# Queries and keys turned by transposing DMAs, and maxima over 1024 keys from two double banks

## The chip, the core and the metric

One core of a Trainium2 chip runs the whole kernel in one launch. Its engines work side by side, each through its own list of instructions, and meet at semaphores: TensorE (PE; PEld is its weight load), VectorE (DVE), ScalarE (ACT), GpSimd (POOL), and SyncE (SP), which here only issues DMAs. The metric is the device time of the kernel in microseconds; lower is better.

## What is computed

A transformer layer on 8 sequences of 1024 tokens of width 256: layer norm, attention with 16 heads of 16 channels (rotary embedding on the last 256 tokens), a residual; then layer norm, a mixture of 16 experts in which each expert takes its 128 best tokens of a sequence, a shared expert, a residual. The change touches the attention alone:

```python
q = (x @ wq + bq); k = x @ wk; v = x @ wv + bv        # [8, 16 heads, 1024, 16]
q, k = apply_rope(q, k, cos, sin)                     # in bfloat16
scores = einsum('bhqd,bhkd->bhqk', q, k) / 4
out = softmax(scores) @ v @ wo + bo
```

## The kernel before

The attention runs first (until about 1510 us), then the shared expert, then the others. All instructions of an engine stand in one order that is written out by hand in the code, in steps. A batch (one sequence) has 64 steps, numbered S = 0 to 63; V counts them over all batches. Four heads make a group; a group and one half of its 1024 queries make a unit of 8 steps, one for each tile of 128 keys. QUAD = 32 channels are kept for a head, of which 16 hold the query or key and three more hold the negative of the row's maximum, split into three bfloat16 parts, so that the turned scores come out of the matmul already less their maximum.

Each step V does four things.

- Rows of scores (`score_rows`, L742): for 128 queries of one head against 512 keys, into one of the three `ring` banks. VectorE takes the maximum over the 512 keys (`maximum`, L460). Four rows a step, 32 a unit, LEAD = 12 steps ahead of their use. VectorE joins the two halves of the keys (`join_halves`, L467), POOL splits the maxima into `QP` (`split_maxima`, L299).
- Turned scores (`score_turned`, L754): four a step, one for each head j (called ex 0 to 3), 128 keys against 512 queries, into the rotating banks `rot`; ScalarE takes their exp into `PR` (L575).
- Values (`weigh_values`, L765): the products of step V - 2, four heads on four column strips, into the bank `pv`.
- Work beside (`beside`, L81, by the table `BESIDE`): projections q, k, v of the next batch, the output projection and gates of the batch before, transposes of activations (`xt`, `aot`, `x2t`), and the transposes of queries and keys: `qT` turns a group's queries or keys by eight TensorE transposes (L707) that ScalarE copies out (L596), `q2` turns a unit's queries again once their maxima are in (L714, L605). In every eighth step the finished output of a unit is turned too (`ot`). ScalarE copies a unit's `pv` bank out before that (`evacuate`, L627).

A head's matmul of scores uses 32 rows of the array (`tile_position`, strip j), and in each half of a step PE issues two rows of scores and two turned scores for four different heads:

```python
score_rows(m); score_rows(m + 1)          # heads 2, 3
score_turned(V, 0); score_turned(V, 1)
weigh_values(V - LAG)
score_rows(m + 2); score_rows(m + 3)      # heads 0, 1
score_turned(V, 2); score_turned(V, 3)
for item in beside(V): fill(item)
```

All exps and all work beside share the rotating banks in one sequence (`ORDER`, L102): item n uses bank n % ROT, ROT = 4, and PE waits until ScalarE has emptied item n - ROT (`bank`, L659). A row of scores m waits in the same way for the maximum of row m - RING (L749). SP loads and stores whole batches as soon as their semaphores allow (L250).

Of the kernel before, what the change touches and what calls it, by code (L numbers as in the profile page):

```python
# [43 lines left out]
def attention(nc, d, ident, SC, B):  # L44
# [12 lines left out]
    ROT = 4  # L57
    RING = 3
    P_STEPS = 3
    LAST = B * STEPS  # L60
    CHECKS = 32 * UNITS * B
# [4 lines left out]
    BESIDE = {0: (-1, "aot", 0, 0), 1: (-1, "aot", 1, 0), 2: (0, "qT", 2, 0), 3: (0, "v", 7), 4: (0, "qT", 2, 1),  # L66
              5: (-1, "proj", 0), 6: (0, "q2", 1), 7: (-1, "aot", 0, 1), 8: (-1, "aot", 1, 1), 9: (-1, "proj", 1),
              10: (-1, "proj", 2), 11: (-1, "proj", 3), 12: (-1, "proj", 4), 13: (-1, "proj", 5), 14: (0, "q2", 2),
# [9 lines left out]
    FIRST = {61: (1, "v", 0), 52: (1, "v", 1), 53: (1, "v", 2), 55: (1, "v", 3), 56: (1, "qT", 1, 0), 57: (1, "qT", 1, 1),  # L78
             58: (1, "v", 4), 59: (1, "v", 5), 60: (1, "v", 6), 62: (1, "q2", 0)}

    def beside(V):  # L81
# [7 lines left out]
        if S in table:  # L89
# [4 lines left out]

    HEAD = ([("xt", 0, h, half) for half in range(2) for h in range(KH)]
            + [(n, 0, i) for i in TILES for n in ("q", "k")]
            + [("qT", 0, 0, 0), ("qT", 0, 0, 1), ("bo",)])
# [13 lines left out]
    def check(m):  # L111

        unit, n = m // 32, m % 32
        return unit, (2, 3, 0, 1)[n % 4], n // 4 % 2, 4 * (unit % 2) + n // 8

    ctx = ExitStack()
    with ctx:
# [6 lines left out]
        identb = sb("identb", [P, P], BF16)  # L124
# [19 lines left out]
        QP = [sb(f"QP{n}", [P, TT, NH, QUAD], BF16) for n in range(2)]  # L144
        KP = sb("KP", [P, TT, NH, QUAD], BF16)
# [10 lines left out]
        MX = sb("MX", [P, 2, 2, 4, 4], F32)  # L156
# [12 lines left out]
        rt1 = sb("rt1", [P, ROPE_TILES, NH, HD], BF16)  # L169
        rt2 = sb("rt2", [P, ROPE_TILES, NH, HD], BF16)  # L170
# [31 lines left out]
        maxima_ready = sem("maxima_ready")  # L202
# [15 lines left out]
        def _(sp):  # L218
# [28 lines left out]

            sp.dma_start(XR[:], rows("x", 0)).then_inc(xr_in, 16)
            load_next(1)
            for b in range(B):  # L250
                if b:
                    store_x1(b - 1)
                if b + 2 < B:
                    load_next(b + 2)
                if b:
                    store_xn2(b - 1)
                    sp.wait_ge(x1_out, 16 * b)
                    sp.wait_ge(xn2_out, 16 * b)
                    sp.dma_start(XR[:], rows("x", b)).then_inc(xr_in, 16)
# [6 lines left out]
        def _(pool):  # L266
# [9 lines left out]
            def rope(b):  # L276

                pool.wait_ge(rot_done, done(("k", b, 7)))
                pool.wait_ge(q_biased, TT * b + 2)
                for n, A in enumerate((QP[b % 2], KP)):  # L280
                    if n:
                        pool.wait_ge(rope_done, 2 * b + 1)
                    a = A[:, TT - ROPE_TILES:TT, :, 0:HD]
                    h = HD // 2

                    def over(c, lo, hi):
                        return c[:, :, lo:hi].unsqueeze(2).to_broadcast([P, ROPE_TILES, NH, hi - lo])
                    nc.gpsimd.tensor_tensor(rt1[:], a, over(cosb, 0, HD), ALU.mult)
                    nc.gpsimd.tensor_tensor(rt2[:, :, :, 0:h], a[:, :, :, h:HD], over(sinb, 0, h), ALU.mult)
                    own.inc(nc.gpsimd.tensor_tensor(rt2[:, :, :, h:HD], a[:, :, :, 0:h], over(sinb, h, HD), ALU.mult))  # L290
                    own.wait(pool)
                    nc.gpsimd.tensor_tensor(a, rt1[:], rt2[:], ALU.add).then_inc(rope_done, 1)

            def clear_maxima(b):

                own.inc(nc.gpsimd.memset(QP[b % 2][:, :, :, HD:HD + 3], 0.0))
                own.wait(pool)
# [124 lines left out]
        def _(dve):  # L422
# [87 lines left out]
            for V in range(-LEAD, LAST):  # L510
# [6 lines left out]
                if m < CHECKS:  # L517
                    maximum(m + 2)
                    maximum(m + 3)
                    if m % 32 == 28:  # L520
                        join_halves(m // 32)
# [837 lines left out]
```

## Time and profile before

| what | us |
|---|---|
| time before, median of 3 runs | 2411.47 (2410.88 to 2412.66) |
| the profiled execution: its time | 2413.08 |
| its span, first to last instruction | 2411.3 |
| PE, DVE, ACT, POOL busy | 2272.7, 1864.4, 1630.3, 1098.7 |
| maxima (L464), 2048 of 512 keys | 1283.6 busy |
| exps (L575), 2048 | 1121.6 busy |

The busy times are unions over the span. PE's is of little use by itself, since matmuls overlap and their ends are modelled; starts are what to compare. VectorE and ScalarE are busy nearly all the time in the attention and half of it later.

### The profile page before, as it was taken

The page shows a single profiled execution, that of the slowest core. Times are in us where ns is not written, and L with a number is a line of the kernel's source. Part 1 is how long each engine was busy: PE and PEld are TensorE (multiplying, and loading weights), DVE is VectorE, ACT ScalarE, POOL GpSimd, SP SyncE. Part 2 cuts the span into 40 slices and gives each one's busy share as a digit, 9 for nine tenths or more (in the row PEclk, how much of TensorE's full clock was granted, in tenths as well). Part 3 has the DMA queues.
Part 4 walks back from the last instruction along what each step waited for, and adds up shares of the span by engine and source line. Part 5 has one row for each costly group of instructions (what it writes and reads, how often), then busy time and mean ns, then how long its engine had stood idle before and what let it go on. Part 6 is the DMA issues. An engine that isn't in the chain of part 4 may idle for free. (4 is left out here: it accounts for less than half of the span.)

```text
span 2411.3 us, 43902 instructions
## 1 busy us (share of the span) xinstructions
PE 2272.7 (94%) x16398; PEld 1335.3 (55%) x16398; DVE 1864.4 (77%) x3234; ACT 1630.3 (68%) x3168; POOL 1098.7 (46%) x1321
## 2 busy tenths in 40 slices
PE   5899999999999999999999997899997999999996
PEld 4233334334334334343344323788886888888886
DVE  5999999999999999999999993556564554555553
ACT  2699999999999999999999986323232343433332
POOL 4152573673573563663663342000004666666664
PEclk8799999999999999999999999899998999999998
DMA  2000011010020010010010010423223445454443
GB/s 76 1 19 1 1 36 36 1 54 19 4 67 3 19 53 1 19 54 1 19 36 1 19 36 27 140 79 104 79 70 90 103 109 113 83 114 111 105 96 36
DMA packets 104363, 122.74 MB, mean 51 GB/s; under 512 B 7553, under 2 KB 91393, under 8 KB 104193
## 3 DMA queue, kind: packets, MB, share of 16 engines
q1 hardware_dynamic: 79616, 86.90, 11.4%
q0 software_dynamic: 24576, 33.57, 8.0%
q8 instruction: 107, 1.75, 0.3%
q14 instruction: 64, 0.52, 0.1%
HBM read 78.50 MB, written 41.94 MB: 50 GB/s over the span
## 5 line engine op out<-in xcount | busy, mean ns | idle before, releaser
L464 DVE TENSOR_REDUCE sb_MX<-ring 128x1 f32<-128x512 f32 x2048 | 1283.6, 684 | 88.7 <-PE ring L751 66.1
L575 ACT ACTIVATE sb_PR<-rot 128x512 f32<-128x512 f32 x2048 | 1121.6, 620 | 89.1 <-PE rot L762 78.0
L773 PE MATMUL pv<-sb_PR,sb_VA 128*32 128x512 f32 x4096 | 547.1, 606 | 2.9 <-ACT sb_OT L630 0.6
L751 PE MATMUL ring<-sb_KT,sb_QT 32*128 32x512 bf16 x2048 | 508.3, 391 | 41.6 <-DVE sb_MX L464 29.0
L751 PEld LDWEIGHTS ring<-sb_KT,sb_QT 32*128 32x128 bf16 x2048 | 125.2, 91 | 619.5 <-DVE sb_MX L464 551.8
L762 PE MATMUL rot<-sb_QT,sb_KT 32*128 32x512 bf16 x2048 | 422.7, 386 | 1.6
L1064 ACT ACTIVATE ex_GL<-ex_gu 128x512 f32<-128x512 f32 x128 | 76.5, 598 | 347.2 <-PE ex_gu L41 345.0
L1131 DVE TENSOR_TENSOR ex_HF<-ex_GL,ex_gu 128x512 f32<-128x512 f32 x128 | 87.5, 683 | 250.7 <-ACT ex_GL L1064 250.7
L985 POOL TENSOR_TENSOR ex_pool_scratch<-identity 128x1 f32<-128x1 f32 x96 | 35.1, 366 | 459.8 <-POOLq L828 314.7
L1028 POOL DMA_INDIRECT out<-ex_YS,ex_rows_out x128 | 209.2, 1634 | 44.1 <-issue 43.5
L39 PE MATMUL ex_gu<-ex_XH,weights_high 128*128 128x512 f32 x512 | 200.4, 391 | 2.4 <-DVE ex_XL L1123 2.4
L40 PE MATMUL ex_gu<-ex_XL,weights_high 128*128 128x512 f32 x512 | 200.0, 391 | 0.0
L41 PE MATMUL ex_gu<-ex_XH,weights_low 128*128 128x512 f32 x512 | 199.9, 390 | 0.0
L366 POOL TENSOR_TENSOR sb_RD<-sb_AR,sb_minus_one 128x16 f32<-128x16 f32 x64 | 186.2, 2909 | 19.3 <-ACT sb_AR L610 19.3
L305 POOL CAST sb_QP<-sb_MX 128x16 bf16<-128x16 f32 x64 | 16.4, 256 | 378.6 <-DVE sb_MX L470 378.6
L1064 ACT ACTIVATE sh_GL<-sh_gu 128x512 f32<-128x512 f32 x64 | 38.2, 597 | 177.2 <-PE sh_gu L41 177.2
L39 PE MATMUL ex_y<-weights_high,ex_HH 128*128 128x256 f32 x512 | 148.2, 289 | 2.9 <-DVE ex_HL L1135 2.9
L773 PEld LDWEIGHTS pv<-sb_PR,sb_VA 128*32 128x32 f32 x4096 | 80.7, 108 | 124.4 <-issue 70.3
L40 PE MATMUL ex_y<-weights_low,ex_HH 128*128 128x256 f32 x512 | 145.5, 284 | 0.0
L41 PE MATMUL ex_y<-weights_high,ex_HL 128*128 128x256 f32 x512 | 145.5, 284 | 0.0
L1006 POOL DMA_INDIRECT ex_XG<-xn,ex_rows_in x128 | 126.0, 985 | 40.2 <-issue 39.6
L39 PE MATMUL rot<-sb_WH,sb_XH 128*128 128x256 f32 x384 | 129.0, 336 | 14.7 <-DVE sb_XL L458 4.8
(165 smaller groups left out, 4279.3 us busy)
## 6 DMA issues: line engine op xcount, KB each, us to landing
sb_XA<-x SPq DMA_DIRECT2D x8, 1024.0 KB, 5.7
sb_XR<-x SPq DMA_DIRECT2D x8, 1024.0 KB, 5.5
out<-sb_XR SPq DMA_DIRECT2D x8, 1024.0 KB, 4.5
xn<-sb_XN SPq DMA_DIRECT2D x8, 1024.0 KB, 4.5
sh_XG<-xn SPq DMA_DIRECT2D x16, 512.0 KB, 5.4
sh_X<-out SPq DMA_DIRECT2D x16, 512.0 KB, 4.9
weights<-WgT SPq DMA_DIRECT2D x16, 512.0 KB, 4.2
weights<-WuT SPq DMA_DIRECT2D x16, 512.0 KB, 5.9
```

What stands on the lines that cost most here:

```text
L39: nc.tensor.matmul(out, a_hi, b_hi, start=first, stop=False)
L40: nc.tensor.matmul(out, a_hi, b_lo, start=False, stop=False)
L41: return nc.tensor.matmul(out, a_lo, b_hi, start=False, stop=last)
L366: own.inc(nc.gpsimd.tensor_tensor(RD[:], AR[:, :, HD], minus_one[:], ALU.pow))
L464: nc.vector.reduce_max(MX[:, unit % 2, half, j, qt % 4:qt % 4 + 1], ring[m % RING][:], AX.X).then_inc(ring_done, 1)
L575: out = nc.scalar.activation(PR[V % P_STEPS][:, j, :], R[:], ACT.Exp, scale=0.25)
L751: nc.tensor.matmul(ring[m % RING][:], QT[g][r, P * qt:P * qt + P], KT[g][r, 512 * half:512 * half + 512], start=True, stop=True, tile_posi ...
L762: nc.tensor.matmul(R[:], KT[g][r, P * kt:P * kt + P], QT[g][r, 512 * qh:512 * qh + 512], start=True, stop=True, tile_position=(r.start, 0) ...
L773: out = nc.tensor.matmul(pv_bank[head(j), :], VA[b % 2][:, kt, 4 * g + j, :], PR[V % P_STEPS][:, j, :], start=(kt == 0), stop=(kt == TT - 1))
L1006: nc.gpsimd.indirect_dma_start(out=XG[k % 2][:, t, :], out_offset=None, in_=d["xn2"], in_offset=bass.IndirectOffsetOnAxis(ap=rows_in[:, b: ...
L1028: nc.gpsimd.indirect_dma_start(out=d["out"], out_offset=bass.IndirectOffsetOnAxis(ap=rows_out[:, b:b + 1], axis=0), in_=YS[k % 2][:, t, :] ...
L1064: nc.scalar.activation(GL[f % 2][:], gu[f % 2][:, 0, 0:N], ACT.Gelu).then_inc(gelu_ready, 1)
```

## The change

- A `ring` bank becomes a double bank: `score_rows` writes the two halves of the keys by two matmuls, one after the other, and `maximum` runs over 1024. There are 16 rows a unit and two a step, so one in each half step: of head 2 or 3 in the first, of head 0 or 1 in the second. `join_halves` goes.
- Two double banks (RING = 2) take four of the eight PSUM banks; the rotating banks become three (ROT = 3).
- The items `qT` and `q2` go from TensorE and ScalarE. SP issues transposing DMAs instead: `turn_qk` for the keys and queries of a group, `turn_whole` for the queries of a unit with their maxima. `QP` and `KP` are laid out by group for that.
- SP's other loads and stores get places among the turns, in the order of the steps. Rope on POOL runs tile by tile (16 instructions for 8). ScalarE's first key copy, POOL's split and clear, and PE's scores wait for turns.

```diff
-    ROT = 4
-    RING = 3
+    ROT = 3
+    RING = 2
-    CHECKS = 32 * UNITS * B
+    CHECKS = 16 * UNITS * B
     (BESIDE and FIRST lose their "qT" and "q2" entries; the others keep their steps)
+    TURN = {47: 0, 51: 1, 55: 2}
     def check(m):
-        unit, n = m // 32, m % 32
-        return unit, (2, 3, 0, 1)[n % 4], n // 4 % 2, 4 * (unit % 2) + n // 8
+        unit, n = m // 16, m % 16
+        return unit, (2, 0, 3, 1)[n % 4], 4 * (unit % 2) + n // 4
-        ring = [ctx.enter_context(nc.psum_tensor(f"ring{i}", [P, 512], F32)) for i in range(RING)]
+        ring = [ctx.enter_context(nc.psum_tensor(f"ring{i}", [P, 2, 512], F32)) for i in range(RING)]
+            def turn_qk(b, g):
+                sp.wait_ge(rope_done, 4 * (b + 1))
+                sp.wait_ge(q_biased, TT * (b + 1))
+                sp.wait_ge(rot_done, done(("k", b, TILES[-1])))
+                if b:
+                    sp.wait_ge(rot_done, done(("ex", (b - 1) * STEPS + 16 * g + 15, 3)))
+                for A, to in ((KP, KT), (QP[b % 2], QT)):
+                    sp.dma_start_transpose(to[g][:].rearrange("p (t c) -> p t c", c=P),
+                                           A[:, g].rearrange("p t j c -> p (t j c)")).then_inc(qk_turned[g], 16)
+            def turn_whole(unit):
+                b, n = unit // UNITS, unit % UNITS
+                g, qh = n // 2, n % 2
+                sp.wait_ge(parts_ready, unit + 1)
+                sp.dma_start_transpose(QT[g][:, 512 * qh:512 * qh + 512].rearrange("p (t c) -> p t c", c=P),
+                                       QP[b % 2][:, g, 4 * qh:4 * qh + 4].rearrange("p t j c -> p (t j c)")
+                                       ).then_inc(q_whole[n], 16)
+            for g in range(G):
+                turn_qk(0, g)
+            turn_whole(0)
+            for V in range(LAST):
+                b, S = V // STEPS, V % STEPS
+                if S % 8 == 4 and V // 8 + 1 < UNITS * B:
+                    turn_whole(V // 8 + 1)
+                if S in TURN and b + 1 < B:
+                    turn_qk(b + 1, TURN[S])
+                if S == 2 and b:
+                    turn_qk(b, G - 1)
+                if S == 21 and b:
                     store_x1(b - 1)
+                if S == 25 and b + 2 < B:
                     load_next(b + 2)
+                if S == 38 and b:
                     store_xn2(b - 1)
+                if S == 45 and b:
+                    load_rest(b)
+                pool.wait_ge(qk_turned[g], 32 * (b + 1))        (split_maxima)
+                    if b and i == TILES[0]:                     (ScalarE, item k)
+                        for g in range(G):
+                            act.wait_ge(qk_turned[g], 32 * b)
             def score_rows(m):
-                if m % 64 == 0:
-                    pe.wait_ge(rot_done, done(("qT", b, g, 1)))
+                if m % 32 == 0:
+                    pe.wait_ge(qk_turned[g], 32 * (b + 1))
                 if m >= RING:
                     pe.wait_ge(ring_done, m - RING + 1)
-                nc.tensor.matmul(ring[m % RING][:], QT[g][r, P * qt:P * qt + P], KT[g][r, 512 * half:512 * half + 512],
-                                 start=True, stop=True, tile_position=(r.start, 0)).then_inc(ring_full, 1)
+                for half in range(2):
+                    out = nc.tensor.matmul(ring[m % RING][:, half, :], QT[g][r, P * qt:P * qt + P],
+                                           KT[g][r, 512 * half:512 * half + 512], start=True, stop=True,
+                                           tile_position=(r.start, 0))
+                out.then_inc(ring_full, 1)
             def score_turned(V, j):
-                    pe.wait_ge(rot_done, done(("q2", b, unit % UNITS)))
+                    pe.wait_ge(q_whole[unit % UNITS], 16 * (b + 1))
             (PE's list of a step)
-                m = 4 * (V + LEAD)
+                m = 2 * (V + LEAD)
                     score_rows(m)
-                    score_rows(m + 1)
                     score_turned(V, 0), score_turned(V, 1), weigh_values(V - LAG)
-                    score_rows(m + 2)
-                    score_rows(m + 3)
+                    score_rows(m + 1)
                     score_turned(V, 2), score_turned(V, 3), beside(V)
```

## Rows read from the trace of the kernel before

**Rows 1.** By stage: us, busy PE PEld DVE ACT POOL, PEclk, DMA share, GB/s

```profile
300.00:1350.00 1050.00, 1022.65 (x8468) 416.22 (x8468) 1001.23 (x1776) 977.37 (x1994) 565.75 (x716) 1.00 0.08 24
```

**Rows 2.** One line's instructions, once a batch (durations in ns; first and last start)

```profile
L296 POOL MEMSET sb_QP<- x6: 669/670/672, 286.5 to 1170.0; 128x384 bf16 x6
```

**Rows 3.** Timeline of PE, one step: start us, us, engine line, operation

```profile
703.13 0.39 PE L751 MATMUL ring<-sb_KT,sb_QT 32*128 32x512 bf16 x2
703.14 0.39 PE L762 MATMUL rot<-sb_QT,sb_KT 32*128 32x512 bf16 x2
703.45 0.38 PE L39 MATMUL rot<-sb_WH,sb_XH 128*128 128x256 f32 x1
703.56 0.19 PEld L40 LDWEIGHTS rot<-sb_WL,sb_XH 128*128 128x128 f32 x1
...
703.91 0.28 PE L39 MATMUL rot<-sb_WH,sb_XH 128*128 128x256 f32 x1
704.03 0.28 PE L40 MATMUL rot<-sb_WL,sb_XH 128*128 128x256 f32 x1
...
704.36 0.39 PE L751 MATMUL ring<-sb_KT,sb_QT 32*128 32x512 bf16 x2
...
704.70 1.07 PE L773 MATMUL pv<-sb_PR,sb_VA 128*32 128x512 f32 x8
705.70 0.39 PE L751 MATMUL ring<-sb_KT,sb_QT 32*128 32x512 bf16 x2
...
706.02 0.66 PE L721 MATMUL rot<-identity,sb_OT 128*128 128x128 f32 x4
```

**Rows 4.** Lines by form, VectorE, 300:1500 us: busy us, mean ns | idle before

```profile
L464 DVE TENSOR_REDUCE sb_MX<-ring 128x1 f32<-128x512 f32 x1678 | 1052.6, 684 | 50.6 <-PE ring L751 31.5
...
L432 DVE BATCH_NORM_STATS2 sb_stats<-sb_XA 128x6 f32<-128x256 f32 x40 | 14.9, 414 | 0.0
...
L484 DVE TENSOR_REDUCE sb_total<-sb_powers 128x8 f32<-128x128 f32 x7 | 1.9, 277 | 0.1
```

**Rows 5.** Timeline, ScalarE behind PE: an exp, the copies of the outputs, two exps

```profile
700.52 0.39 PE L762 MATMUL rot<-sb_QT,sb_KT 32*128 32x512 bf16 x2
...
701.00 0.60 ACT L575 ACTIVATE sb_PR<-rot 128x512 f32<-128x512 f32 x1 [0.21 <-PE rot L762]
...
701.50 0.58 ACT L630 COPY sb_OT<-pv 128x512 f32<-128x512 f32 x1
...
707.16 0.39 ACT L610 COPY sb_AR<-rot 128x272 f32<-128x272 f32 x1
...
707.81 1.09 ACT L575 ACTIVATE sb_PR<-rot 128x512 f32<-128x512 f32 x2
```

**Rows 6.** Timeline, a matmul that waits for its bank: ScalarE's exp, then PE

```profile
1007.09 0.64 ACT L575 ACTIVATE sb_PR<-rot 128x512 f32<-128x512 f32 x1
...
1007.78 0.38 PE L762 MATMUL rot<-sb_QT,sb_KT 32*128 32x512 bf16 x1
```

**Rows 7.** Timeline of PE, the gate's matmuls

```profile
560.87 1.96 PE L734 MATMUL rot<-sb_gw,sb_XT 128*128 128x16 f32 x16
```

**Rows 8.** DMA issues of SP: out<-in, count, KB each, median us to landing

```profile
sb_AO<-wo SPq DMA_DIRECT2D x1, 256.0 KB, 6.3
...
sb_gw<-gwT SPq DMA_DIRECT2D x1, 16.0 KB, 4.4
```

**Rows 9.** Timeline: K's last copy and first scores; POOL's split, first and last step

```profile
40.73 0.37 ACT L593 CAST sb_KP<-rot 128x256 bf16<-128x256 f32 x1 [0.33 <-PE rot L41]
...
44.07 0.39 PE L751 MATMUL ring<-sb_KT,sb_QT 32*128 32x512 bf16 x3 [0.65 <-ACT sb_KT L596]
...
710.70 0.25 POOL L305 CAST sb_QP<-sb_MX 128x16 bf16<-128x16 f32 x1
...
711.95 0.25 POOL L313 CAST sb_QP<-sb_rest 128x16 bf16<-128x16 f32 x1
```

**Rows 10.** One line's instructions: the turned scores, first and last start

```profile
L762 PE MATMUL rot<-sb_QT,sb_KT x2048: 371/385/605, 80.8 to 1478.8; 32*128 32x512 bf16 x187
```

More of the change, by code:

```diff
@@ L143, in attention @@
         AL = sb("AL", [P, KH, T], FR)
-        QP = [sb(f"QP{n}", [P, TT, NH, QUAD], BF16) for n in range(2)]
-        KP = sb("KP", [P, TT, NH, QUAD], BF16)
+        QP = [sb(f"QP{n}", [P, G, TT, 4, QUAD], BF16) for n in range(2)]
+        KP = sb("KP", [P, G, TT, 4, QUAD], BF16)
         QT = [sb(f"QT{g}", [P, T], BF16) for g in range(G)]
@@ L201, in attention @@
         rot_done = sem("rot_done")
-        maxima_ready = sem("maxima_ready")
+        qk_turned = [sem(f"qk_turned{g}") for g in range(G)]
+        q_whole = [sem(f"q_whole{n}") for n in range(UNITS)]
         parts_ready = sem("parts_ready")
@@ L249, in _ @@
             load_next(1)
-            for b in range(B):
-                if b:
+            for g in range(G):
[10 more added lines that the diff above has]
+                if S == 21 and b:
@@ L279, in rope, with over @@
                 pool.wait_ge(q_biased, TT * b + 2)
+                h = HD // 2
                 for n, A in enumerate((QP[b % 2], KP)):
[L281 to L292, printed above, removed]
+                    for t in range(ROPE_TILES):
+                        if n or t:
+                            pool.wait_ge(rope_done, 4 * b + 2 * n + t)
+                        a = A[:, :, TT - ROPE_TILES + t, :, 0:HD]
+                        def over(c, lo, hi):
+                            return c[:, t, lo:hi].unsqueeze(1).unsqueeze(1).to_broadcast([P, G, 4, hi - lo])
+                        r1, r2 = rt1[:, t], rt2[:, t]
+                        nc.gpsimd.tensor_tensor(r1, a, over(cosb, 0, HD), ALU.mult)
+                        nc.gpsimd.tensor_tensor(r2[:, :, :, 0:h], a[:, :, :, h:HD], over(sinb, 0, h), ALU.mult)
+                        own.inc(nc.gpsimd.tensor_tensor(r2[:, :, :, h:HD], a[:, :, :, 0:h], over(sinb, h, HD), ALU.mult))
+                        own.wait(pool)
+                        nc.gpsimd.tensor_tensor(a, r1, r2, ALU.add).then_inc(rope_done, 1)
             def clear_maxima(b):
-                own.inc(nc.gpsimd.memset(QP[b % 2][:, :, :, HD:HD + 3], 0.0))
+                for n in range(UNITS):
+                    pool.wait_ge(q_whole[n], 16 * (b - 1))
+                own.inc(nc.gpsimd.memset(QP[b % 2][:].rearrange("p g t j c -> p (g t j) c")[:, :, HD:HD + 3], 0.0))
                 own.wait(pool)
@@ L301, in split_maxima @@
                 b, g, qh = unit // UNITS, unit % UNITS // 2, unit % 2
-                to = [QP[b % 2][:, 4 * qh:4 * qh + 4, 4 * g:4 * g + 4, HD + n].rearrange("p t j -> p j t") for n in range(3)]
-                whole = MX[:, unit % 2, 0]
-                pool.wait_ge(maxima_ready, unit + 1)
+                to = [QP[b % 2][:, g, 4 * qh:4 * qh + 4, :, HD + n].rearrange("p t j -> p j t") for n in range(3)]
+                whole = MX[:, unit % 2]
+                pool.wait_ge(qk_turned[g], 32 * (b + 1))
+                pool.wait_ge(ring_done, 16 * (unit + 1))
                 own.inc(nc.gpsimd.tensor_copy(to[0], whole))
@@ L592, in empty @@
                     _, b, i = item
-                    out = nc.scalar.copy(KP[:, i, :, 0:HD], R[:, 0:H].rearrange("p (h c) -> p h c", c=HD))
-                elif kind == "qT":
-                    _, b, g, n = item
-                    out = nc.scalar.copy((QT, KT)[n][g][:], R[:].bitcast(BF16))
+                    if b and i == TILES[0]:
+                        for g in range(G):
+                            act.wait_ge(qk_turned[g], 32 * b)
+                    out = nc.scalar.copy(KP[:, :, i, :, 0:HD], R[:, 0:H].rearrange("p (g j c) -> p g j c", g=G, c=HD))
                 elif kind == "v":
@@ L742, in score_rows @@
             def score_rows(m):
-                unit, j, half, qt = check(m)
+                unit, j, qt = check(m)
                 b, g = unit // UNITS, unit % UNITS // 2
-                if m % 64 == 0:
-                    pe.wait_ge(rot_done, done(("qT", b, g, 1)))
+                if m % 32 == 0:
+                    pe.wait_ge(qk_turned[g], 32 * (b + 1))
                 if m >= RING:
```

72 lines of the change are left out of this document (18 added, 54 removed), and 13 rows, old and new, of the table BESIDE.

## The prediction

> **What bounds the kernel now.** I read the busy time by stage first, then the timeline of single steps, then single waits. The stage that matters is the attention loop. There PE, VectorE and ScalarE are busy 97%, 95% and 93% of the time [rows 1], so no engine has room and a shared average decides nothing. A batch (64 steps) takes (1170.0 - 286.5) / 5 = 176.7 us [rows 2], 2.76 us a step. The timeline of one step that carries a projection shows the order on PE [rows 3]: two rows of scores and two turned scores start within 0.01 us of each other, on four different 32-row strips of the array, and the next work starts 0.32 us later; six matmuls of a projection, 0.91 us; again four strips, 0.33; then the values, 1.00. The sum is 2.57 us and nothing waits: PE sets such a step. In a step without work beside, VectorE sets it: four maxima at 1052.6/1678 = 0.627 us, 2.51 us [rows 4].
>
> What doesn't show as a cost yet is the loop between PE and ScalarE through the rotating banks: PE may fill item n when ScalarE has emptied item n-4. With four banks the second turned score of a step (call the four ex0 to ex3) waits, in a step after work beside, for ex2 of the step before, which is done in time. When a bank does bind, the trace shows what follows: the exp ends at 1007.09+0.64 = 1007.73, the matmul starts at 1007.78 [rows 6].
>
> **Part by part: VectorE.** One maximum of 1024 takes the place of two of 512. A small reduction of 128 elements lasts 0.277 us and one of 512 lasts 0.684 [rows 4], so 1.06 ns an element, and a maximum of 1024 should come every 0.627 + 0.543 = 1.17 us: 2.34 us a step instead of 2.51, or 64 x 0.17 = 10.9 us of VectorE a batch (the eight joins of halves that go too are tiny).
>
> **The transposes that go.** 16 turning items a batch leave PE and ScalarE, so 16 of the 62 steps with work beside lose it. After the change 18 of the 64 steps have none, 36 have one item, 8 have one more (the output's transposes, ot), 2 have the gate's matmuls (lg).
>
> **What PE pays.** Before, the four matmuls of a half step lie on four strips. After, both halves of one row of scores lie on the same strip (j is 2 or 3 in the first half, 0 or 1 in the second), so they can't be two of the four. Nothing in the trace shows two on one strip. Nearest: two matmuls of 256 columns that use the same rows start 0.12 apart [rows 3], so 512 columns hold them for 0.24. From below it is 0 (all four side by side as now), from above the whole 0.39 of one matmul [rows 3]. I take 0.24, as columns stream one after another there too: 0.48 a step.
>
> The Trainium skill ("TensorE: Matmul & The Clock Gate", Part 3) says that a weight load overlaps matmuls in flight only when its row group differs. In this trace it doesn't hold: the load of L40 starts at 703.56, 0.11 after the matmul of L39 on all 128 rows and well before that matmul's end [rows 3]. By the rule the second half's load would stand open once in the loop below; with L40's 0.19 as its price, 64 x 8 x 0.19 = 97 us more, 2698.
>
> **What three banks pay.** Now item n waits for n-3. After a step with one item beside, ex1 waits for ex3 of the step before; after one with none, for ex2; with ot too, for ot. The pieces: matmul start to exp start 0.48 on an idle ScalarE (700.52 to 701.00); exp after exp 1.09 - 0.60 = 0.49; an exp 0.60; the copy of ot 0.39 [rows 5]; bank free to matmul 0.05 [rows 6]. From ex2's start to the next ex1:
> none beside 0.48 + 0.60 + 0.05 = 1.13; one item 0.48 + 0.49 + 0.60 + 0.05 = 1.62; item and ot 0.48 + 0.49 + 0.49 + 0.39 + 0.05 = 1.90.
> PE by itself would be there after 1.22 + 0.24 = 1.46 in a projection step, so it waits. Behind ex1 stand, in PE's order, the values (0.33 later, 1.00 long), the next row of scores (0.24), then ex2: 1.57 us. So a step takes 2.70, 3.19 or 3.47 us. The gate's 16 matmuls last about 1.9 [rows 7], and PE itself sets those: 0.32 + 1.9 + 0.24 + 1.57 = 4.03. Once a unit ScalarE also copies the finished values between ex2 and ex3 (0.58, in spacing about 0.47 [rows 5]); in 5 of 8 units the step has work beside and pays it. A batch: 18 x 2.70 + 36 x 3.19 + 8 x 3.47 + 2 x 4.03 + 5 x 0.47 = 201.7 us, 25.0 more than now. VectorE's 2.34 is below every one of these steps, and its statistics (two of 0.41 [rows 4] in each of eight steps) raise it to 3.16 there, which the banks' steps and the second double bank take in: its gain is off the path.
>
> The six middle batches pay 150 us. First and last have 1478.8 - 80.8 - 6 x 176.7 = 337.8 us now [rows 10]; counted the same way (first: 35 steps without, 23 with one item, 6 with two, 0.9 of copies; last: 38, 21, 2, two gates, 1.4, less 12 x 0.24 where no scores are left, and 1.57 to the last item) they take 189.6 + 184.7 = 374.3: 36.5 more.
>
> **The transposing DMAs.** No row shows one. SP's plain DMAs land 4.4 to 6.3 us after issue [rows 8]; a transposing one may cost less or much more. For each unit, the last maximum ends some 0.3 us into the fourth step before its scores, the split on POOL takes 1.5 [rows 9], and 4 x 3.15 - 1.9 = some 10.5 us are left to land. So I cost them at nothing in the loop; the cover is that time. The turns of a whole group are due six steps after their last input, or more. At the start there is no cover: now K's last copy ends at 41.10 and scores start at 44.07 [rows 9]; after, two DMAs land at 46 to 48, and rope has twice the instructions: +2 to +5, I take 3.5.
>
> **Waits and order.** ScalarE's first k of a batch waits for four turns (all its exps stand behind it), POOL's split and clear wait for turns as well: all were issued 8 steps or more before. SP's stores and loads now stand behind the turns in its queue; the load of the residual comes at step 45 and lands about two steps later, when POOL asks for it. Bias and key copies keep their element counts. These cost nothing while DMAs land in about 6 us.
>
> **Sum.** 150 + 36.5 + 3.5 = 190. The profiled execution took 2413.08, 1.6 above the median, with a span of 2411.3; on the median 2411.5 + 190 = 2601 us. With 0.39 on the strip it is 64 x 8 x 0.15 = 77 more, 2678.
>
> **Rivals.**
> Faster: both halves of a row run beside the turned scores and ScalarE is ahead of the banks; then VectorE's 10.9 us a batch come through: 2411.5 - 8 x 10.9 + 3.5 = 2328. It decides if ex2-to-ex1 stays below 1.1 us. For it: VectorE sets the light steps now. Against: the 0.48 and 0.60 are measured on an idle ScalarE, and shorter steps need them shorter. 7%.
> Strip free, banks bind: every step 0.24 less, 185.8 us a batch, 2411.5 + 8 x 9.1 + 3.5 = 2488. 6%.
> Strip binds, banks don't (the bank wait overlaps something I don't see): 32 projections take 2.57 + 0.48 = 3.05, 12 steps with four transposes beside some 2.54 (0.4 in place of 0.91; the four last 0.66 with the end that the next work overlaps [rows 3]), ot 0.4 eight times, the gates 4.04, 18 steps VectorE's 2.34: 181.5 us a batch, so 2411.5 + 8 x 4.8 + 3.5 = 2453. 8%.
> DMAs too slow: two groups (four turns of 256 KB) stand ahead of a unit's turn in SP's queue; from the last key copy (about step 46.3) to that unit's scores (step 56) there are 9.7 x 3.15 = 30.6 us. It decides when a turn of 256 KB takes over (30.6 - 6.3) / 4 = 6.1 us. If each 128 KB costs a full 6.3 with no overlap, 4 x 12.6 + 6.3 - 30.6 = 26 us a batch, seven times: 2784. For it: no trace shows such a DMA, and 16 a batch share one queue with loads. Against: plain ones of 16 and of 256 KB land within 2 us of each other [rows 8]. 13%.
> The Trainium skill ("VectorE: DVE Perf Modes", The three transpose paths) gives 1309 ns for a DMA transpose of 128x128 against 390 on TensorE; as a price per block that is 10.5 us for 256 KB, an estimate from that page, and 2601 + 7 x 16.5 = 2717. No run here shows it.
>
> **How the numbers follow.** Forecast 66% (2550 to 2680 by itself: 0.1 us a step is 51 us), rivals as above. The range 2480 to 2720 takes in the free strip, the 0.39, and the milder half of slow DMAs. Faster than 0.2% (about what a measurement of this kernel can tell from no change) 8%, within 3%, slower 89%.
>
> **What would show it.** Right: steps of about 2.7 without and 3.2 with work beside; ring matmuls of one pair 0.2 apart; PE waiting for exp ahead of L762's successor 0.2 to 0.8 us a step; VectorE near 80% busy with spacing 1.17. Wrong: PE's scores waiting for a DMA (slow turns), steps of 2.4 (banks don't bind), a granted clock below 1.0 in the loop.

## The result and the profile after

| | before | after |
|---|---|---|
| time, median (range), us | 2411.18 (2408.59 to 2412.66) | 2640.18 (2622.61 to 2678.13) |
| ratio, 95% interval | | 1.0925 (1.0868 to 1.0981) |
| profiled execution, time and span | 2413.08, 2411.3 | 2622.61, 2620.8 |
| a batch in the steady loop | 176.7 | 201.1 |

The change makes the kernel 9% slower. The ratios here and below leave out executions more than 1.5% above the fastest of their kernel, here the one of 2678.13 us. The profiled execution of after is the fastest of four; why the others scatter is taken up below.

The loop by stage, in the columns of [rows 1]:

```profile
300.00:1350.00 1050.00, 990.88 (x6844) 350.66 (x6844) 827.92 (x846) 811.84 (x1644) 508.16 (x671) 0.98 0.15 36
```

VectorE and ScalarE are no longer full: 79% and 77% instead of 95% and 93%. PE still shows 94%, though it starts a fifth fewer matmuls (6844 against 8468): as said under the table of before, its busy time is of little use. Two rows of lines, the counterparts of [rows 2] and [rows 10] (duration min/median/max in ns, first and last start in us):

```profile
L330 POOL MEMSET sb_QP<- x6: 652/660/671, 312.4 to 1332.1; 128x384 bf16 x6
```

```profile
L767 PE MATMUL rot<-sb_QT,sb_KT x2048: 371/385/630, 83.4 to 1686.5; 32*128 32x512 bf16 x187
```

The memsets give (1332.1 - 312.4) / 5 = 203.9 us a batch on average. From the first turned score of each batch to that of the next it is 192.7, 201.1, 201.1, 210.7, 201.1, 205.8 and 201.1: a steady 201.1, a shorter first one, and two longer ones. The lengths of single steps, here and below, are counted from a step's ex2 to the next step's ex2. Now the inside of one step. PE from one half step to the next, beside it ScalarE in the same stretch, the counterparts of [rows 3], [rows 5] and [rows 6]:

```profile
858.82 0.39 PE L754 MATMUL ring<-sb_KT,sb_QT 32*128 32x512 bf16 x1
858.83 0.39 PE L767 MATMUL rot<-sb_QT,sb_KT 32*128 32x512 bf16 x2
859.05 0.37 PE L754 MATMUL ring<-sb_KT,sb_QT 32*128 32x512 bf16 x1
859.35 0.39 PE L39 MATMUL rot<-sb_WH,sb_XH 128*128 128x256 f32 x1
...
860.05 0.28 PE L41 MATMUL rot<-sb_WH,sb_XL 128*128 128x256 f32 x1
860.27 0.38 PE L754 MATMUL ring<-sb_KT,sb_QT 32*128 32x512 bf16 x1
860.27 0.39 PE L767 MATMUL rot<-sb_QT,sb_KT 32*128 32x512 bf16 x1
860.49 0.38 PE L754 MATMUL ring<-sb_KT,sb_QT 32*128 32x512 bf16 x1
860.63 0.39 PE L767 MATMUL rot<-sb_QT,sb_KT 32*128 32x512 bf16 x1
860.95 0.64 PE L778 MATMUL pv<-sb_PR,sb_VA 128*32 128x512 f32 x4
```

```profile
858.83 0.09 PEld L754 LDWEIGHTS ring<-sb_KT,sb_QT 32*128 32x128 bf16 x1
```

```profile
858.30 0.59 ACT L598 ACTIVATE sb_PR<-rot 128x512 f32<-128x512 f32 x1
859.49 1.09 ACT L598 ACTIVATE sb_PR<-rot 128x512 f32<-128x512 f32 x2 [0.60 <-PE rot L767]
860.46 0.38 ACT L624 COPY sb_VA<-rot 128x256 f32<-128x256 f32 x1
860.94 0.60 ACT L598 ACTIVATE sb_PR<-rot 128x512 f32<-128x512 f32 x1
```

Four things are to be seen. Ex1 of the next step (860.63) starts 0.05 after the second of the two exps has ended (859.49 + 1.09 = 860.58), so the three banks bind just where the prediction put it. The two halves of a row of scores start 0.23 apart on their strip (858.82 and 859.05). The weight load of the second half is not what holds it: it starts at 858.83, 0.01 after the first half (the line of PEld), so the 2698 us with open weight loads do not come about. And between, ScalarE was idle for 0.60 us: each engine waits for the other in turn.

The maxima, the exps and the turned scores by form from 300 to 1500 us (busy us, mean ns, idle before), against [rows 4]:

```profile
L499 DVE TENSOR_REDUCE sb_MX<-ring 128x1 f32<-128x1024 f32 x756 | 911.3, 1222 | 253.0 <-PE ring L754 251.2
L598 ACT ACTIVATE sb_PR<-rot 128x512 f32<-128x512 f32 x1509 | 817.2, 603 | 242.1 <-PE rot L767 231.2
L767 PE MATMUL rot<-sb_QT,sb_KT 32*128 32x512 bf16 x1510 | 410.3, 388 | 55.1 <-ACT sb_PR L598 50.3
```

VectorE now waits for PE (253 us against 51), ScalarE as well. PE's own idle time ahead of the turned scores, 50.3 us in 377 steps, is only 0.13 us a step, less than the 0.2 to 0.8 that the prediction gave as a sign: PE's wait shows in the starts (ex0 at 860.27, ex1 at 860.63), while matmuls already started still count as busy. The turning DMAs (count, median us from issue to landing) and PE's first rows of scores, against [rows 8] and [rows 9]:

```profile
sb_QT<-sb_QP SPq DMA_TRANSPOSE x96, 2.4
sb_KT<-sb_KP SPq DMA_TRANSPOSE x32, 3.3
```

```profile
49.59 1.04 PE L754 MATMUL ring<-sb_KT,sb_QT 32*128 32x512 bf16 x4 [4.49 <-DMA sb_QT<-sb_QP]
```

The first line mixes the 64 turns of a unit (128 KB, 2.4 us) with 32 of a group's queries (256 KB); the second has the 256 KB of a group's keys. They land sooner than the two plain DMAs of [rows 8], which come from outside SBUF. At the start PE does wait 4.5 us for them; in the loop its matmuls never wait for them.

### The profile page after: what moved, and what is told of

The parts are those of the page before. It is cut to its first block and busy times, and to the rows that moved or that the text cites. A ratio compares the mean times of both kernels' runs of the same rounds, so it can differ in the third digit from the quotient of the medians.

```text
span 2620.8 us, 41313 instructions
## 1 busy us (share of the span) xinstructions
PE 2425.0 (93%) x15630; PEld 1318.1 (50%) x15630; DVE 1800.5 (69%) x2145; ACT 1571.7 (60%) x3040; POOL 1108.9 (42%) x1385
## 5 line engine op out<-in xcount | busy, mean ns | idle before, releaser
L499 DVE TENSOR_REDUCE sb_MX<-ring 128x1 f32<-128x1024 f32 x1024 | 1230.8, 1221 | 352.2 <-PE ring L754 350.2
L598 ACT ACTIVATE sb_PR<-rot 128x512 f32<-128x512 f32 x2048 | 1105.2, 603 | 332.9 <-PE rot L767 319.7
L767 PE MATMUL rot<-sb_QT,sb_KT 32*128 32x512 bf16 x2048 | 560.2, 391 | 87.4 <-ACT sb_PR L598 81.1
L754 PE MATMUL ring<-sb_KT,sb_QT 32*128 32x512 bf16 x2048 | 583.8, 390 | 13.1 <-DVE sb_MX L499 7.4
L778 PE MATMUL pv<-sb_PR,sb_VA 128*32 128x512 f32 x4096 | 558.9, 619 | 2.3
L754 PEld LDWEIGHTS ring<-sb_KT,sb_QT 32*128 32x128 bf16 x2048 | 112.1, 93 | 534.5 <-DVE sb_MX L499 249.1
L767 PEld LDWEIGHTS rot<-sb_QT,sb_KT 32*128 32x128 bf16 x2048 | 134.7, 91 | 274.8 <-ACT sb_PR L598 260.5
L39 PE MATMUL ex_gu<-ex_XH,weights_high 128*128 128x512 f32 x512 | 201.1, 393 | 2.4 <-DVE ex_XL L1126 2.4
```

What stands on the lines that cost most here:

```text
L39: nc.tensor.matmul(out, a_hi, b_hi, start=first, stop=False)
L499: nc.vector.reduce_max(MX[:, unit % 2, j, qt % 4:qt % 4 + 1], ring[m % RING][:].rearrange("p a n -> p (a n)"), AX.X).then_inc(ring_done, 1)
L598: out = nc.scalar.activation(PR[V % P_STEPS][:, j, :], R[:], ACT.Exp, scale=0.25)
L754: out = nc.tensor.matmul(ring[m % RING][:, half, :], QT[g][r, P * qt:P * qt + P], KT[g][r, 512 * half:512 * half + 512], start=True, stop= ...
L767: nc.tensor.matmul(R[:], KT[g][r, P * kt:P * kt + P], QT[g][r, 512 * qh:512 * qh + 512], start=True, stop=True, tile_position=(r.start, 0) ...
L778: out = nc.tensor.matmul(pv_bank[head(j), :], VA[b % 2][:, kt, 4 * g + j, :], PR[V % P_STEPS][:, j, :], start=(kt == 0), stop=(kt == TT - 1))
```

## The experiments

**The parts one by one.** Each part of the change was put into the kernel before by itself.

Three rotating banks alone:

```diff
-    ROT = 4
+    ROT = 3
```

> The kernel before with three rotating banks in place of four (one PSUM bank stays unused), nothing else. If the loop through three banks is a cost by itself: a step with work beside takes 1.62 from ex2 to the next ex1 and 1.33 on to ex2, 2.95 us where it took 2.5 to 2.6; 62 of 64 steps have work beside here, so a batch takes some 195 us in place of 176.7 and the kernel some 2555 us. If the loss of the changed kernel comes from the two matmuls on one strip or from the DMAs, and three banks are enough: 2411 to 2420.

Measured: 2576.19 us (2567.9 to 2578.29), ratio 1.0661 (1.0641 to 1.068). A batch takes 196.8 us, a step with one item 2.94, one with the output's transposes and a projection 3.37, one with gates 3.54 as before. The item's step was meant to be 2.95. So the banks alone cost 165 us, 20.1 in each steady batch. Of the 21 us above the total expected, half lie in the six middle batches (1.8 each above 195). The rest is mostly at the end: up to the last turned score the last batch is 24.9 longer than in the kernel before (18 were expected), with 27 us at half clock about its end, and what follows is 3.3 longer.

One strip for both rows of a half step, with the single banks and 512 keys of before:

```diff
-        return unit, (2, 3, 0, 1)[n % 4], n // 4 % 2, 4 * (unit % 2) + n // 8
+        return unit, (2, 0, 3, 1)[n // 2 % 4], n % 2, 4 * (unit % 2) + n // 8
```

> The kernel before, with its rows of scores issued in another order: the two of a half step are the two halves of the keys of one head, on one 32-row strip, where they were two heads on two strips. Four rotating banks, three single ring banks and maxima of 512 stay. If one strip holds two matmuls one after the other: 0.22 more in each half step, which steps with a projection (32 a batch) pay in full and steps bound by VectorE not at all, so some 14 us a batch, 2510 to 2525 us; the second matmul of a pair starts 0.22 after the first. If the strip is free: 2411.

Measured: 2529.26 us (2518.69 to 2545.28), ratio 1.0486 (1.0436 to 1.0536); a batch of 190.4 us, 13.7 more than before, and projection steps of 2.97 for 2.55. The strip has a price with four banks too: in a projection step 0.42, so 0.21 a half step. Three of the batches were 2.2 to 5.5 us longer still, which had not been expected; see the clock below.

The DMA turns alone, with four banks, three single ring banks and maxima of 512. ScalarE and PE lose qT and q2; the rest of the loop is the kernel before. Written as an edit of the changed kernel:

```diff
     TURN = {47: 0, 51: 1, 55: 2}
     (turn_qk, turn_whole and the layout by group as in the change; BESIDE without qT and q2)
-    ROT = 3
-    RING = 2
+    ROT = 4
+    RING = 3
     (score_rows, check, maximum and join_halves as in the kernel before)
```

> The kernel before with the DMA turns alone: queries and keys turned by SP's transposing DMAs, rope and SP's order as in the changed kernel, but four rotating banks, three single ring banks and maxima of 512. If the DMAs are hidden and the items that they replace held ScalarE and PE up (steps of 2.6 to 3.2 with qT beside): 4 to 6 us a batch less, 2370 to 2385 us. If the DMAs or the longer list on SP cost something by themselves: 2411 or more.

Measured: 2399.57 us (2398.87 to 2400.75), ratio 0.9942 (0.9925 to 0.9959). Faster than both kernels, but by 14 us where 28 to 43 were expected. Its loop by stage, in the columns of [rows 1]:

```profile
300.00:1350.00 1050.00, 994.83 (x8010) 384.71 (x8006) 1015.60 (x1800) 938.49 (x1926) 580.04 (x770) 1.00 0.19 42
```

VectorE is busy 97% of it: a batch fell from 176.7 to 174.4 us and no further. Of the 16 steps that lost an item, eight took 2.49 to 2.52 us with it and take as long without: that is the length of VectorE's four maxima (2.51), so the item had not been what held them.

Banks and strip together, without the turns: double banks, maxima of 1024, three banks, and the transposes still on TensorE.

```diff
-    ROT = 4
-    RING = 3
+    ROT = 3
+    RING = 2
     (score_rows, check and maximum as in the change; qT and q2 stay in BESIDE)
```

> The kernel before with the double banks alone: maxima of 1024 from two double banks, three rotating banks, but queries and keys turned by TensorE and copied by ScalarE as before. If the loss of the changed kernel is the loop of three banks with two matmuls on a strip, all 62 steps with work beside pay it (3.1 us each): some 210 us a batch, 2650 to 2670 us, slower than the changed kernel's 2622 to 2678. If the DMAs are what costs in the changed kernel: faster than it, 2400 to 2500.

Measured: 2700.38 us (2680.31 to 2704.22), ratio 1.1166 (1.1116 to 1.1215), a batch of 209.9. The batch is the one expected, the time is 30 us above; three of the batches have falls of the clock, as below, and take 213.2 to 219.1. Banks 20.1 and strip 13.7 add up to 33.8; it is 33.2. The turns then save 209.9 - 201.1 = 8.8 us a batch, four times what they save with four banks: a step that loses its item is 0.48 shorter there (3.12 to 2.64), because its successor's ex1 then waits for ex2 and no longer for ex3.

**VectorE.** The changed kernel, with maxima over the first half of the keys:

```diff
-  ring[m % RING][:].rearrange("p a n -> p (a n)")
+  ring[m % RING][:, 0, :]
```

> The changed kernel with each maximum taken over the first 512 of its 1024 keys only: VectorE does half of that work, everything else stays (the maximum is then that of half the keys). If VectorE is off the path of the steps: a batch stays at 201 us, steps stay 2.64 and 3.12, the kernel stays within 2620 to 2680 us. If VectorE's 1.17 a maximum and two banks still hold PE up: steps get shorter, under 198 us a batch, under 2600 us.

Measured: 2634.43 us (2628.19 to 2663.29), ratio 1.0962 (1.0917 to 1.1006), with VectorE busy 483 us of the same stretch:

```profile
300.00:1350.00 1050.00, 980.98 (x6846) 351.11 (x6846) 483.00 (x845) 811.88 (x1645) 506.96 (x670) 0.98 0.15 36
```

All steady batches are 201.1 as before this edit. What the longer maxima gain, or could gain, lies wholly off the path of the changed kernel.

**Where the strip is paid.** In the changed kernel the exp starts 0.67 after its matmul (858.83 to 859.49), not 0.48 as in [rows 5]. Two readings: the turned scores are slower beside the strip, or they are done and handed over behind the second half, which stands ahead of them in PE's order. So, the turned scores first:

```diff
-                    score_rows(m)
                 (turned scores 0 and 1)
+                    score_rows(m)
                 (values)
-                    score_rows(m + 1)
                 (turned scores 2 and 3)
+                    score_rows(m + 1)
```

> The changed kernel with the turned scores issued ahead of the row of scores in each half step. The changed kernel's trace shows turned scores that start beside the first half of a row but whose exp starts 0.67 after them, not 0.48. If they are handed over only when the matmul ahead of them in program order has ended: the exp starts 0.48 after again, the values come 0.54 after ex1 instead of 0.33, the two cancel, steps of 2.67 and 3.16, some 203 us a batch, 2630 to 2690 us. If the 0.67 has another cause (ScalarE, the semaphore): it stays, and steps grow to 2.85 and 3.35, some 214 us a batch, over 2700 us.

Measured: 2616.4 us (2602.27 to 2629.26), ratio 1.0828 (1.0787 to 1.0868); undisturbed batches of 197.1. PE and ScalarE in one step:

```profile
700.70 0.39 PE L767 MATMUL rot<-sb_QT,sb_KT 32*128 32x512 bf16 x2
700.71 0.60 PE L754 MATMUL ring<-sb_KT,sb_QT 32*128 32x512 bf16 x2
701.24 0.66 PE L688 MATMUL rot<-identity,sb_AO 128*128 128x128 f32 x4
701.83 0.82 PE L767 MATMUL rot<-sb_QT,sb_KT 32*128 32x512 bf16 x2
702.27 0.60 PE L754 MATMUL ring<-sb_KT,sb_QT 32*128 32x512 bf16 x2
702.80 1.06 PE L778 MATMUL pv<-sb_PR,sb_VA 128*32 128x512 f32 x8
703.79 0.39 PE L767 MATMUL rot<-sb_QT,sb_KT 32*128 32x512 bf16 x2
```

```profile
701.12 1.09 ACT L598 ACTIVATE sb_PR<-rot 128x512 f32<-128x512 f32 x2 [0.54 <-PE rot L767]
```

The exp now starts 0.42 after its matmul and before the second half ends (700.71 + 0.60 = 701.31): the hand-over goes in PE's order. But most of the gain is given back: both halves now start behind ex1's wait (at 702.26, the second of the merged row), and the values 0.54 after it, so ex1 to ex2 is 703.79 - 702.26 = 1.53 us where the changed kernel has 1.30. The strip is paid once a half step, ahead of the hand-over or ahead of the values. The forecast of 203 us a batch was too high by 6.

**The strip in place.** A double bank that holds 512 keys of two heads, on two strips, with one reduction that gives both maxima. Three banks, double banks and turns stay:

```diff
-                r = head(j)
-                for half in range(2):
-                    out = nc.tensor.matmul(ring[m % RING][:, half, :], ...)
+                for n in range(2):
+                    r = head(j + n)
+                    out = nc.tensor.matmul(ring[m % RING][:, n, :], ...)
-                nc.vector.reduce_max(MX[..., j, ...], ring[m % RING][:].rearrange("p a n -> p (a n)"), AX.X)...
+                nc.vector.reduce_max(MX[..., half, j:j + 2, ...], ring[m % RING][:], AX.X)...
     (and the order of heads and the join of the halves on VectorE, as before)
```

> The changed kernel, but a double bank now holds 512 keys of two heads (two strips) instead of 1024 keys of one head (one strip), in the old order of heads (2, 3 then 0, 1); one reduction gives both maxima, and the join of the halves is back on VectorE. Three banks, two double banks and the DMA turns stay. Theory, the strip costs what two matmuls on one strip cost (about 0.23 us a half step): steps become those of three banks alone, 2.50 without, 2.94 with one item, 3.36 with the output's transposes, 3.54 with gates, so 188 us a batch and 2515 to 2540 us, and no fall of the clock in the loop as in the kernel with three banks alone. Rival, the price lies in the double bank or in fewer, longer maxima that hold TensorE, not in the strip: steps stay at 2.64 and 3.12, 201 us a batch, 2605 to 2680. In between, if VectorE's reduction to two outputs is longer than 1.17 us in spacing: light steps of 2.5 to 2.6, 2540 to 2560.

Measured: 2481.71 us (2475.0 to 2487.88), ratio 1.0282 (1.0251 to 1.0313), batches of 185.9, steps of 2.43 without and 2.92 with an item; faster than expected (2515 to 2540 us, 188 a batch, 2.50 without an item). PE, ScalarE and the line of maxima (300 to 1350 us):

```profile
854.31 0.39 PE L763 MATMUL ring<-sb_KT,sb_QT 32*128 32x512 bf16 x2
854.32 0.39 PE L776 MATMUL rot<-sb_QT,sb_KT 32*128 32x512 bf16 x2
854.64 0.38 PE L39 MATMUL rot<-sb_WH,sb_AH 128*128 128x256 f32 x1
```

```profile
854.78 1.09 ACT L607 ACTIVATE sb_PR<-rot 128x512 f32<-128x512 f32 x2 [0.58 <-PE rot L776]
```

```profile
L500 DVE TENSOR_REDUCE sb_MX<-ring 128x2 f32<-128x1024 f32 x717 | 861.3, 1222 | 144.2 <-PE ring L763 134.8
```

All four start within 0.01 us again, the exp comes 0.46 later, and two maxima of 512 last as long as one of 1024 (1222 ns). So the strip, not the double bank, costs 201.1 - 185.9 = 15.2 us a batch, and two thirds of the loss (158 of 229 us) are undone without giving up the double banks. It also shows what the long reduction is worth once it counts: a step without an item takes 2.43 us, which four single maxima (2.51) would not allow.

**The bank loop at two banks.**

```diff
-    ROT = 3
+    ROT = 2
```

> The changed kernel with two rotating banks in place of three: item n waits for n-2. If the loop between PE and ScalarE sets every step, its arithmetic must hold here too: without work beside ex1 waits for ex3 of the step before (0.67 + 0.49 + 0.60 + 0.05 = 1.81, and 1.30 on: 3.11 us), with a projection it waits for that item, which itself waits for ex2 (1.32 + 0.91 + 0.14 + 0.39 + 0.05 = 2.8, and 1.30: 4.1 us); some 240 us a batch, 2890 to 2960 us. If the banks are a small part: under 2700 us.

Measured: one execution, 3438.27 us. Where the clock is full, the steps are 3.12 without, 4.07 with an item and 4.55 with the output's transposes; but the clock is full for only a part of the loop:

```profile
300.00:1350.00 1050.00, 889.64 (x4700) 292.05 (x4692) 579.21 (x585) 586.59 (x1132) 334.36 (x441) 0.77 0.10 24
```

The step lengths at full clock bear the loop out; the total, for which a full clock was taken, is missed by some 500 us.

**The clock.** The two long batches of the changed kernel each hold a stretch in which the granted clock is 0.5 (1.2 GHz). The first begins within a row of the gates' matmuls, the second (1243.64) 0.4 us after the end of one. PE at the first, and the stretches around it (columns of [rows 1]):

```profile
829.53 2.62 PE L736 MATMUL rot<-sb_gw,sb_XT 128*128 128x16 f32 x16
832.08 0.60 PE L754 MATMUL ring<-sb_KT,sb_QT 32*128 32x512 bf16 x1
```

```profile
829.50:830.60 1.10, 1.10 (x11) 1.07 (x10) 0.96 (x1) 0.93 (x2) 1.10 (x2) 1.00 1.10 204
830.60:854.50 23.90, 23.33 (x102) 9.20 (x102) 10.37 (x11) 10.39 (x23) 2.92 (x8) 0.50 0.07 13
```

The 23.9 us at 1.2 GHz lengthened their batch by 9.6 us, the 10.3 us at 1243.6 theirs by 4.7. The next two kernels ask whether the gates are the cause. First, the two gate steps (S = 47, 48) moved apart:

```diff
-  47: (-1, "lg", 0), 48: (-1, "lg", 1), 51: (1, "v", 0),
+  47: (-1, "lg", 0), 48: (1, "v", 0), 49: (-1, "lg", 1),
```

> The changed kernel with the two gate items, which stood in steps 47 and 48, in steps 47 and 49, and the projection of the first values (step 51) between them in step 48. The granted clock falls to half in the changed kernel at steps 47 to 49 of some batches and nowhere else in the loop. If two gates next to each other let it fall: no fall, 2603 to 2615 us, runs within some 5 us. If the fall doesn't hang on that place: as the changed kernel, 2620 to 2680 us, with falls.

Measured: 2663.67 us (2638.19 to 2690.65), ratio 1.1005 (1.0967 to 1.1043). The clock falls at S = 48 or 50 in four of the middle batches. Second, half of the matmuls of each gate step:

```diff
-                        for h in range(KH):
-                            out = nc.tensor.matmul(R[...], XT[:, h, ...], gw[:, h, :], start=(h == 0), stop=(h == KH - 1))
+                        out = nc.tensor.matmul(R[...], XT[:, 0, ...], gw[:, 0, :], start=True, stop=True)
```

> The changed kernel, with the gate's logits taken over one half of the channels only: 4 matmuls of 16 columns in each of the two gate steps of a batch instead of 8 (the other half of the sum is left out). In the changed kernel TensorE's granted clock falls to 0.5 in the loop twice, 0.7 us after the first gate matmul of a step (829.53, fall at 830.6) and in the same place at 1243.6. Theory A, the row of gate matmuls brings the falls: none is left between batch 1 and batch 6, all of the steady batches take 201.1 less 2 x 0.8 = 199.5 us, and the time is 2600 to 2612 us with little scatter. Rival B, the longer steps as such (TensorE waiting for banks everywhere) bring them and the gate step is only the last straw: falls remain near the gates or move to the steps with ot, batches of 204 to 210 remain, 2615 to 2670.

Measured: 2612.05 us (2605.57 to 2624.87), ratio 1.0813 (1.0792 to 1.0834). The gate's step shrinks to 3.13, the batches to 199.4, and one fall is left in the middle batches, again at S = 47:

```profile
1048.00:1050.20 2.20, 2.20 (x20) 1.08 (x12) 1.92 (x2) 1.63 (x4) 2.20 (x2) 1.00 1.10 227
1050.20:1070.70 20.50, 19.93 (x87) 6.15 (x86) 10.45 (x11) 10.14 (x23) 2.42 (x7) 0.50 0.11 20
```

Neither theory stands: fewer gate matmuls bring fewer falls in this trace, not none. In the six middle batches, the falls are at the gates in every kernel of three or four rotating banks with both halves on one strip (one strip alone, banks and strip together, after and its variants) and once in the kernel with two heads in a bank; in before and in the kernels with three banks alone or turns alone there are none. What decides whether a given gate step brings one stays open. Of these 20 falls, four begin within a row of gate matmuls and the others 0.2 to 1.3 us after the end of one.

The clock also spoils a comparison of totals: in the profiled executions of the kernels with turned scores first, gates apart and half gates, it stays at 1.2 GHz from about 50 us to 166 to 174 us, in the changed kernel's to 100. Their first batch takes 217 us instead of 193, so these kernels are to be compared by their later batches.

**A version that beats both.** With four banks and the turns, eight steps carry the output's transposes and an item and still take 2.94 to 3.33 us. Their items go a step on (one a step back), some pushing their neighbours on, into places that the turns left empty:

```diff
-  3: (0, "v", 7), ... 11: proj 3, 12: proj 4, 13: proj 5, ... 19: xt, 20: xt, 21: xt, 23: xt, ... 27: k 7, ... 59: v 5, 60: v 6
+  4: (0, "v", 7), ... 12: proj 3, 13: proj 4, 14: proj 5, ... 20: xt, 21: xt, 22: xt, 23: xt, ... 28: k 7, ... 60: v 5, 61: v 6
```

> The kernel before with the DMA turns alone (four rotating banks, three single ring banks, maxima of 512), and with the items that stood in the steps with the output's transposes (S = 3, 11, 19, ... 59) moved by one or two steps into places that the turns left empty. With the DMA turns alone a step with both takes 2.94 to 3.33 us, 3.04 on average, and a step with one item 2.55; no row shows the output's transposes alone, taken as 2.55 to 2.65. Theory, room that the turns leave is worth something where the banks still make a loop with two items: 8 x 0.4 to 0.5 less 8 x 0.05, so 171.0 to 171.8 us a batch instead of 174.4 and 2374 to 2382 us. Rival, VectorE (four maxima of 0.627 and its statistics) sets the sum of neighbouring steps, and the short steps give back what the long ones lose: 174 us a batch, 2395 to 2402.

Measured: 2398.47 us (2396.26 to 2401.3), ratio 0.9949 (0.9932 to 0.9966). The rival's time, but not for its reason. Six of the eight steps came down to 2.57 to 2.60 (S = 35 to 2.87, S = 3 stayed at 3.26), while S = 24, in which the first projection of the next batch stands, went from 3.34 to 4.06 in two of the middle batches and to 5.2 to 5.6 in the other four. POOL and PE in one of these:

```profile
673.66 1.27 POOL L358 TENSOR_TENSOR sb_XL<-sb_XT,sb_XH 128x512 fp32r<-128x512 f32 x1
```

```profile
675.07 0.36 PE L39 MATMUL rot<-sb_WH,sb_XH 128*128 128x256 f32 x1 [1.46 <-POOL sb_XL L358]
```

The transposes of the activations had been moved too, and POOL's split of them came late. PE's wait is 1.46 or 1.47 us in all six; the four longer ones are those in which the granted clock falls to 0.5 for 3.4 us within that step (675.80 here). With these four back in their places:

```diff
-  20: xt, 21: xt, 22: xt, 23: xt
+  19: xt, 20: xt, 21: xt, 23: xt
```

> The kernel with the output's transposes alone, with the four transposes of the activations (xt) put back to S = 19, 20, 21 and 23. In the run before it, the step S = 24 took 5.30 us instead of 2.65: its projection started at 675.07, when POOL's split of the activations (1.27 us, two of them in a row) ended at 674.92; the other steps came out as the theory had it. Theory, that wait alone hid the gain: S = 24 is back at 2.65, one step with ot and xt is 2.94 again, so 174.1 - 2.65 + 0.4 = 171.9 us a batch and 2374 to 2382 us. Rival, VectorE's sum over neighbouring steps sets the batch: 174 us, 2395 to 2402.

Measured: 2386.95 us (2382.08 to 2387.11), ratio 0.9894 (0.9877 to 0.991), a batch of 172.5: the theory's mechanism, and 0.6 us a batch short of its size. The expectation took 2.65 for S = 24, but that step was 3.34 with the turns alone and is 3.34 again: 174.1 - 1.96 + 0.36 = 172.5. This is the fastest kernel here, 1.1% below before. It keeps the change's transposing DMAs and leaves its double banks out.

## Why the prediction was right, point by point

The forecast was 2601 us in a range of 2480 to 2720; 2640.18 lies in it, on the predicted side, and the mechanism named as likeliest is the one that the trace and the single parts show.

- **Three banks: right.** After a step with an item, ex1 starts 0.05 us after the exp of that step's ex3 has ended. Steps measured against those forecast: 2.64 (2.70) without an item, 3.12 (3.19) with one, 3.95 (4.03) with gates, and 0.5 for the copy of the finished values. Three banks alone cost 20.1 us a batch.
- **One strip: right in size, wrong in place.** The prediction put 0.24 us of PE's order ahead of ex2. The halves do start 0.23 apart, but the turned scores start beside the first half and don't wait for the second; what waits is the hand-over: 0.67 from matmul to exp in place of 0.48, and ex1 to ex2 is 1.30 in place of 1.57. The two errors nearly cancel in the sum of a step (0.19 more, 0.27 less): that the steps came out within 0.08 is in part luck. The Trainium skill ("TensorE: Matmul & The Clock Gate", Part 3) states that matmuls start and end strictly in program order. By the ends, as the exps show them here and with the turned scores first, the trace agrees; by the starts it doesn't: at 858.83 two turned scores start 0.22 before the second half of the row of scores that stands ahead of them.
- **The step with a projection and the output's transposes: too short.** 3.47 forecast, 3.76 measured. The prediction let only ex1 wait; here the projection itself waits for ex2's bank (0.67 + 0.60 + 0.05 after ex2's start) and is 0.91 long, so PE comes late by itself, ex0 and ex1 start together beside the first half (2.23 after ex2), and the second half stands ahead of the values: 1.53 to the next ex2, not 1.30. With transposes as the item it is 3.44. Seven such steps cost 2 us a batch more, which the other steps, most of them some 0.06 shorter, more than balance: 201.1 for 201.7.
- **VectorE off the path: right.** Halving its maxima changes no step.
- **DMA turns at nothing in the loop: right.** 2.4 and 3.3 us to landing, against a cover of some 10.5. The rival of slow DMAs needed over 6.1 us for 256 KB and falls. At the start the first turned score comes 2.6 later (3.5 forecast), although PE's first rows of scores come 5.5 later than in [rows 9].
- **The rival of a free strip** was given 185.8 us a batch and 2488 us. The kernel with two heads in a bank is that case: 185.9 and 2482.
- **What the sum lacked: the clock.** On the profiled execution the span grew by 209.5 us against 190. The steady batches give 6 x 24.4 = 146.4 (150 forecast), the start 2.6 (3.5), the first and last batch, counted to the last turned score as in the forecast, 18.8 + 25.7 = 44.5 (36.5); the two falls add 14.3 and what follows the last turned score 1.8. At 1.2 GHz ran 17 us of the first batch and 16 of the last, against 13 and none in the kernel before; at 0.40 us each, the price of the fall above, that is an estimated 8 us, as much as these two batches exceed the forecast by. The prediction named a clock below 1.0 in the loop only as a sign of error, and the sign came (0.98); it gave the clock no term. That the other three executions are longer fits the same cause: the one of 2647.99 us has a mean clock of 0.952 against 0.965, so (0.965 - 0.952) x 2635 / 0.5 = some 68 us more at half clock for 25.4 us more time, 0.37 us each, near the fall above (9.6 / 23.9 = 0.40). Those executions have no trace, so this is argued and not shown.

## What to carry to other kernels

When a change takes buffers from a ring that two engines pass between them, write the round trip out (start to hand-over, the queue ahead, the work, the release) and compare it with the step; here a fourth bank was worth 20 us a batch while the busy times of all engines said nothing of it. The longer reduction came into its own here only when what fills its buffer stayed side by side on the array: two heads in one double bank kept the 1222 ns and spared the strip. And place moved work where its consumers, POOL's split here, still have their time, or the step that gains pays it back elsewhere.

## What was not expected of the hardware

- Two matmuls of 512 columns on one strip of 32 rows start 0.23 us apart, while matmuls on other strips that come later in the order start ahead of the second (858.83 against 859.05). Their results are handed on in order: exp 0.67 us after the start behind the second half, 0.42 ahead of it.
- A reduction of 128x1024 to two maxima lasts as long as one to a single maximum, 1222 ns.
- A transposing DMA from SBUF to SBUF lands in 2.4 us (128 KB) and 3.3 us (256 KB), with plain ones into SBUF at 4.4 (16 KB) and 6.3 (256 KB) in [rows 8].
- The granted clock falls to 0.5 in mid-loop, most often in a row of the gates' matmuls of 16 columns or up to 1.3 us behind one, and stays there for 3 to 27 us. In the kernel in which POOL's split comes late it falls for 3.4 us (675.8 to 679.2 and in three more of the six middle batches) in the step S = 24, after PE has waited 1.46 us for POOL. With two rotating banks it averages 0.77 from 300 to 1350 us. The Trainium skill ("TensorE: Matmul & The Clock Gate", A second HAM failure mode: psum-queue depth-cycling) states that cycling through PSUM banks can leave TensorE idle so often that its clock swings between the two levels. The kernel with two banks agrees; the one with three banks alone, where ex1 waits in most steps at a clock of 1.00, doesn't, and what tells the two apart no run here shows.
